# A node and edge kernel's first stage: the steps between two sort passes moved, and the last rows normalised in one go

## The reference

```python
h = jnp.maximum(_layernorm(x, axis=-1), 0.0)
# inside _L0_gnn_ref(h, rbf=attr32, pij=attr3, dij=attr5, ..., idx_i=src, idx_j=dst):
def _resmlp(x, w1, b1, w2, b2, wout):
    h = x + jnp.dot(_silu(jnp.dot(_silu(x), w1) + b1), w2) + b2
    return jnp.dot(_silu(h), wout)
gs = jnp.dot(rbf, w_rs)
gp = jnp.dot(rbf, w_rp)[:, None, :] * pij[:, :, None]
gd = jnp.dot(rbf, w_rd)[:, None, :] * dij[:, :, None]
xx = _resmlp(x, ...[0])
xs = _resmlp(x, ...[1])[idx_j]      # xp with [2], xd with [3]
s = xx + jax.ops.segment_sum(gs * xs, idx_i, num_segments=n)
p = jax.ops.segment_sum(gp * xp[:, None, :], idx_i, num_segments=n)
d = jax.ops.segment_sum(gd * xd[:, None, :], idx_i, num_segments=n)
pa, pb = jnp.split(jnp.dot(p, w_pp), 2, axis=-1)
da, db = jnp.split(jnp.dot(d, w_pd), 2, axis=-1)
y = s + (pa * pb).sum(-2) + (da * db).sum(-2)
return x_before + _resmlp(y, ...[4])
```

## Time and profile before

| | us |
|---|---|
| median of 3 runs | 1217.9 |
| the runs | 1210.91 to 1219.04 |
| the profiled execution, time | 1216.09 |
| the profiled execution, span of the core | 1214.3 |
| TensorE busy in it | 1099.7 |
| ScalarE busy in it | 733.2 |
| VectorE busy in it | 705.0 |
| GpSimd busy in it | 460.3 |

### The profile page before, as it was taken

How to read it: one execution, slowest core, us unless ns; L and a number is a source line. 1 busy time by engine, 2 the same in 40 slices (tenths; PEclk the granted TensorE clock), 3 DMA queues, 4 the chain that set the end, 5 groups by cost and what they waited for, 6 DMA issues and landing times.

```text
span 1214.3 us, 22950 instructions
## 1 busy us (share of the span) xinstructions
PE 1099.7 (91%) x6361; PEld 721.9 (59%) x6361; DVE 705.0 (58%) x2443; ACT 733.2 (60%) x1373; POOL 460.3 (38%) x425
## 2 busy tenths in 40 slices
PE   3677998986888939999999999999988999999998
PEld 2455665664555615666666666666754666666665
DVE  9977677684566405565655666565643444444442
ACT  3456777965777835555555555556535666566654
POOL 3055666215556632655655565565340000000000
PEclk9988999998899979999999999999999999999999
DMA  9276776944665443757666666665437999999984
GB/s 274 94 228 210 229 222 207 319 141 148 197 211 189 161 100 48 80 85 79 67 73 70 67 72 77 69 66 72 90 58 202 279 277 270 267 283 271 270 272 145
DMA packets 269855, 198.49 MB, mean 163 GB/s; under 512 B 166882, under 2 KB 191498, under 8 KB 269631
## 3 DMA queue, kind: packets, MB, share of 16 engines
q1 hardware_dynamic: 231438, 152.34, 45.0%
q0 software_dynamic: 24208, 19.29, 16.3%
q10 hardware_dynamic: 14112, 25.70, 6.0%
HBM read 101.03 MB, written 96.26 MB: 162 GB/s over the span
## 4 chain that ended last, share of the span: by engine, by line
PE 73%; DVE 14%; issue 6%; another core or an unknown queue 2%; DMA 2%; ACT 1%; SPq 1%; POOL 0%; ACTq 0%; POOLq 0%; DVEq 0%
PE quad L1095 7%; PE bank L1109 7%; PE bank L1695 6%; PE quad L1101 5%; PE bank L1705 5%; PE bank L1767 4%; DVE stat L525 4%; PE bank L1737 3%; PE bank L1768 3%; PE quad L844 3%; PE bank L861 3%; DVE picked L654 3%; PE quad L851 2%; DVE onehot L637 2%
## 5 line engine op out<-in xcount | busy, mean ns | idle before, releaser
L1349 POOL DMA_INDIRECT node_sums<-rowout,row_i x98 | 156.7, 1599 | 163.8 <-ACT rowout L1625 141.3
L1016 DVE TENSOR_TENSOR rowout<-bank,xin 128x512 f32<-128x512 f32 x98 | 67.8, 692 | 142.6 <-PE bank L1109 141.7
L470 POOL DMA_INDIRECT edges_by_src<-pay,rank_i x98 | 96.4, 983 | 106.4 <-DVE rank_i L666 52.4
L470 POOL DMA_INDIRECT edges_by_low<-pay,rank_i x98 | 97.6, 996 | 95.4 <-DVE rank_i L666 43.1
L1109 PEld LDWEIGHTS bank<-wo_sb,s 128*128 128x128 f32 x784 | 102.8, 191 | 47.8 <-issue 47.8
L861 PEld LDWEIGHTS bank<-wo_sb,s 128*128 128x128 f32 x720 | 95.9, 196 | 57.9 <-issue 57.9
L1396 DVE SCALAR_TENSOR_TENSOR h<-bank,b_sb,hT 128x512 f32<-128x512 f32 (+1 forms) x75 | 55.5, 740 | 121.2 <-PE bank L1705 105.8
L74 POOL DMA_INDIRECT yin<-node_h,er x98 | 94.8, 967 | 57.9 <-issue 28.9
L654 DVE SCALAR_TENSOR_TENSOR picked<-bank,onehot 128x256 bf16<-128x256 f32 (+1 forms) x196 | 67.5, 388 | 83.0 <-PE bank L817 34.5
L754 ACT ACTIVATE xn<-xin,nbias,rnorm 128x128 f32<-128x128 f32 x216 | 104.1, 493 | 14.2 <-DVE nbias L576 14.2
L861 PE MATMUL bank<-wo_sb,s 128*128 128x128 f32 x720 | 98.2, 280 | 8.4 <-ACT rowout L793 5.8
(11 more groups left out here) (205 smaller groups left out, 2296.1 us busy)
## 6 DMA issues: line engine op xcount, KB each, us to landing
xin<-in_x_dram SPq DMA_DIRECT2D x196, 256.0 KB
node_h<-xn SPq DMA_DIRECT2D x98, 256.0 KB
out_dram<-rowout ACTq DMA_DIRECT2D x98, 256.0 KB
node_sums<-rowout SPq DMA_DIRECT2D x90, 256.0 KB
yin<-node_sums SPq DMA_DIRECT2D x53, 256.0 KB, 3.7
yin<-node_sums SPq DMA_DIRECT2D x180, 64.0 KB, 3.2
src_in_every_row<-edge_src_row SPq DMA_DIRECT2D x24, 256.0 KB
border_sums_by_tile<-border_sums SPq DMA_DIRECT2D x24, 256.0 KB
```

The lines of the kernel that those rows point to most:

```text
L470: nc.gpsimd.indirect_dma_start(out=ps.dram, out_offset=bass.IndirectOffsetOnAxis(ap=rank_i[:, t:t + 1], axis=0), in_=pay[:, t, :], in_offs ...
L1349: nc.gpsimd.indirect_dma_start(out=ysum, out_offset=bass.IndirectOffsetOnAxis(ap=row_i[:, t % 2, j:j + 1], axis=0), in_=urow[:, t % 2, j, ...
```

## The change

It has two parts. Between the sort's passes (second pass only): the seven groups of counts move from steps 49 to 52 to half a step earlier each, 48 to 51; VectorE makes the corrections in step 48 instead of 51, reads the counts at the end of step 48 instead of 49, and makes the totals in step 49 instead of 50; TensorE makes the seeds in step 52 ahead of the second layer's matmul instead of behind it; the scatters' pace is counted from one step earlier. The statistics stay in the steps where they were. In the last rows: from step 94 on, ScalarE no longer takes the norms of blocks 95, 96 and 97 one step at a time between the SiLUs, but all at once in step 94, ahead of the second SiLU of block 93. SP stores of block 97 only the rows that are not block 96's, 84 partitions of 128, and no longer waits for the store before it.

```diff
-                self.chunks, self.scatters, self.alone, self.dram, self.width = chunks, chunks, alone, dram, width
+                self.chunks, self.alone, self.dram, self.width = chunks, alone, dram, width
...
-                      Pass(1, {48: (0, 7)}, ((49, 0), (49, 1), (50, 0), (50, 1), (51, 0), (51, 1), (52, 0)), 52, 53, (48, 53), by_src, HIGH))
+                      Pass(1, {48: (0, 7)}, ((48, 1), (49, 0), (49, 1), (50, 0), (50, 1), (51, 0), (51, 1)), 52, 53, (48, 53), by_src, HIGH))
...
-                    if b == NB - 1:
-
-                        sp.wait_ge(h_stored[(b - 1) % 4], 16 * ((b - 1) // 4 + 1))
-                    sp.dma_start(xb_view(at(b), htab), xn[:, s, :, :]).then_inc(h_stored[s], 16)
+                    first = (b * BLOCK - at(b).start) // TB
+                    sp.dma_start(xb_view(at(b), htab)[first:P], xn[first:P, s, :, :]).then_inc(h_stored[s], 16)
...
-                    half = 2 * ps.scatters + 5 * t // 6
+                    half = 2 * (ps.chunks - ps.n) + 5 * t // 6
...
-                        if k == max(ps.made_at) + (3 if ps.n else 1):
+                        if k == max(ps.made_at) + (0 if ps.n else 1):
                             corrections(ps)
                     while todo:
                         next_norm_step()
                     if pick:
                         ranks(*pick)
                     for ps in passes:
-                        if k == max(ps.made_at) + 1:
+                        if k == max(ps.made_at) + (0 if ps.n else 1):
                             dve.wait_ge(s_cst, 3)
                             dve.wait_ge(s_count, ps.n + 1)
                             nc.vector.tensor_copy(counts_h[:, 0:ps.width], BANK_COUNT[:, 0:ps.width]).then_inc(s_counts, 1)
-                        if k == max(ps.made_at) + 2:
+                        if k == max(ps.made_at) + (1 if ps.n else 2):
                             totals(ps)
...
-                    norm(k + 1, 0)
-                    norm(k + 1, 1)
-                    norm(k + 1, 2)
+                    if k < NK:
+                        for j in range(TB - 1):
+                            norm(k + 1, j)
+                    elif k == NK:
+                        for b in range(NK + 1, NB):
+                            for j in range(TB):
+                                norm(b, j)
...
-                    norm(k + 1, 3)
+                    if k < NK:
+                        norm(k + 1, TB - 1)
...
                     for ps in passes:
                         counts(ps, k, 0)
+                        if ps.n and k == ps.seeded_at:
+                            seeds(ps)
...
                     for ps in passes:
-                        if k == ps.seeded_at:
+                        if ps.n == 0 and k == ps.seeded_at:
                             seeds(ps)
```

## The result

| | median | lowest to highest | runs |
|---|---|---|---|
| kernel before | 1217.22 us | 1210.91 to 1219.73 | 8 |
| kernel after | 1222.02 us | 1216.11 to 1227.85 | 8 |
| after / before | 1.0047 | 95% interval 1.0026 to 1.0067 | |

The changed kernel is slower by 0.5%, some 5 us, where 6.4 us less were forecast. 1222.0 us lies outside the range of 1204 to 1219 us and on the other side of the kernel before. It is within the 1% that the chances called "the same". The profiled execution of the changed kernel took 1216.11 us with a span of 1214.3 us. Its stretches do.

A forecast was written before the change was run, and what follows sets the result against it. TensorE, busy 91% of the span, was taken as the bound, with time to gain before block 55 and at the edge hand-over. -2.4 - 1.9 - 2.1 = -6.4 us gave 1211.5 us from 1217.9 us; range 1204 to 1219 us.

The forecast's parts named there:

- the same: Whole kernel: measured time within 1%, 12 us, of the kernel before; chance 0.85.
- First place: Between the sort's passes, about 250 to 270 us: counts read and block 55 sooner, -2.4 us, plus -1.9 us of clock.
- The 2.4 us from order and waits: Between the passes: counts earlier -1.5, corrections hidden -2.6, eight statistics on the chain +1.65 us; block 55 at about 264.8 us.
- The clock term: TensorE at block 55: gap shrinks from 3.83 to about 1.9 us, so full clock instead of half, -1.9 us, or 0.
- Second place: Hand-over to the edge stage, 430 to 450 us: first load of sorted edges at 434.25 instead of 436.35 us, -2.1 us.
- the sentence on the scatters' pace: Second pass: last scatter comes one step earlier, but the edge stage waits last for the stores, so 0 us.
- The carrying: From 267 to 436 us: the 4.3 us gained between the passes arrive whole, with no fixed-time wait seen and order unchanged.
- a stall that I had priced at 6.3 us: Stall before 306.23 us: TensorE idle 4.42 us, then at half clock; 6.3 us with the clock's 1.9 us.
- Slower: Rival: earlier scatters load the DMA engines and unnamed stalls grow by 6.3 us each; chance 0.10.
- the case above no change: Rival's case of two grown stalls: 1224.1 us, slower than before; chance 0.04.
- stall by stall count: Unnamed stalls growing 6.3 us each: one gives 1217.8 us, no change; two give 1224.1 us, slower.

The follow-up runs named there:

- the copy of before: The kernel before, unchanged, run again on the chip where it takes 1147 us, to measure noise and get its profile: ratio 1.0009 (0.9991 to 1.0027).
- the late pace: Kernel before with only the second pass's scatters paced from step 55, two steps later, on a chip with unnamed waits: 1201.55 us, 0.9916 of before.
- the spaced kernel: Changed kernel, pace still from step 52, with a 320-column clear and a wait behind each of the second pass's 98 scatters: 1206.63 us, 0.9960 of before.

## Why the prediction was wrong

- **First place, right.** Forecast for reading the counts 253.1 us; measured 249.09 us, which with the 3.77 us that this execution was ahead is 252.9 us. Idle time before it 2.62 us for some 2.3. Block 55 at 260.66, so 264.4 us for 264.8, after a gap of 1.54 us for 1.9. Full clock behind this gap. Together -4.7 us for -4.3 us (-5.2 us on the quiet chip, the copy of before against the changed kernel). The 2.4 us from order and waits measured 2.8 (step 49 to 55: 31.8 us before, 29.0 after), and the same on a second chip with the waits. That the whole came so close is in part luck: from step 55 to 57 the unnamed waits mix in.
- **The clock term** is not as fixed as -1.9 us made it look. From the transposes of block 55 to those of block 56 the fourteen traces with the new first place take 3.7 us each, behind gaps of 1.5 to 2.1 us, always at full clock. The six with the old one all have a gap of 3.8 us, but take 5.4 (the kernel before), 6.4 (its copy on the quiet chip), 5.2, 5.1, 5.4 and, in the kernel with the last rows alone, 3.7 us at full clock. The term is worth 0 to 2.7 us, 1.7 in the pair first compared.
- **The Trainium skill** (TensorE: Matmul & The Clock Gate, Part 1) says that where a switch of the clock falls differs from run to run. The six traces agree.
- **Second place, right.** -2.5 us on both kinds of chip for -2.1 us. All terms had been rows of that very place.
- **The step that failed** is the sentence on the scatters' pace: "the last scatter then comes one step earlier, but what the edge stage waits for last is the stores: 0". It priced the edit by its end, whether the last scatter holds anybody up. In the changed kernel nobody waits for it, that was right. Its price is along the way: the pace was what kept scatters from going out in long unbroken rows, and on the chips with unnamed waits such rows go with late hand-overs from TensorE to ScalarE, VectorE and GpSimd. Alone it costs 0.84% there, 10 us, more than all the rest gains. The steps where it acted are those where the start of the pace makes a difference: a start at 52 holds the scatters back from about step 73 on, one at 53 from about step 67, one at 55 at once (an estimate: tile t's picks are ready at about step 55 + 0.357 t, 98 tiles in 35 steps, and the pace lets it go at step start + 0.417 t), and the step times part just there: 52 and 53 up to step 72, 53 and 55 up to step 67.
- **The carrying.** I had written that I saw no wait on a fixed time and that the order of instructions was unchanged, so 4.3 us would go through. The row that should have stopped me was among mine: 15.6 us of VectorE's waits with no releaser, beside a stall that I had priced at 6.3 us. What moves relative to such waits is not carried through.
- **The rival with the right place.** "Slower" named scatters one step earlier and stalls of unnamed releaser that grow. It had 0.10, and 0.04 for the case above no change, with the argument "the same bytes move". They do: the kernel before moves 269,855 packets and 198.49 MB on both kinds of chip. Its mechanism, load on the DMA engines, is not what the runs show: in the middle of the longest stall they are 7% busy. What they show is the distance at which GpSimd issues scatters. Its stall by stall count was also wrong in kind: ScalarE's waits grow by many small ones (those of rowout went from 4 to 11), not by one or two of 6.3 us.

What stays open: why unbroken indirect scatters slow TensorE's hand-overs, why a third of a microsecond between them is enough, and why one of the chips shows none of it (whether that lies in the chip, or in something else that was running on the others, no run tells). The runs show that spacing removes it; they do not show which part of the chip is shared. The spacing was always made by a clear and a wait for it, so a pause by itself was not tried; the late pace is the only second means, and it brings steps 57 to 72 to 56.2 us, not to the 49.4 us of the spaced kernel.

## What to carry to other kernels

A rule that holds back an engine's issues is not free to move because nobody waits for their end: ask what runs beside them and whether the rule was what kept them apart. Where a trace has waits with no releaser, note which other activity they coincide with, and count any edit that shifts or thickens that activity as a risk with a price. Take the parts of a change apart on more than one chip: here the same kernel gains 0.5% on one and loses 0.4% on another, and neither alone would have shown why.

## What the runs showed of the hardware

- One program took 1147 us on one chip and 1211 to 1217 us on the others. Outside the scatters the step times agree: between steps 47 and 55 the trace of the quiet chip is a constant 36.8 us ahead. Nearly all of the 70 us between the chips arises in the two stretches with scatters.
- On the others, a VectorE instruction waited 31.3 us while 37 indirect scatters went out 1.27 us apart; at 1.63 us apart there was no such wait in 160 us. The DMA engines were 7% busy in the middle of the first case and 69% over steps 57 to 94 in the second. Whether TensorE's matmuls themselves end late or only the news of them, the trace cannot tell, since their ends are modelled.
- GpSimd's own issue of a 128-row scatter takes 0.97 us, and 0.30 us lie between two.
- TensorE kept its full clock behind gaps of 1.5 to 2.1 us in fourteen traces; behind 5.11 us it had the low one. Behind one and the same gap of 3.8 us it had the low clock at once in four traces, at full speed for the first transposes and low right after in one, and full throughout in one.
